# The column of negated maxima turned into a row: float32 transposes in place of float32 products with the identity

## What is computed

```
xn = _layernorm(x, gamma_media, beta_media)          # x: 6404 context rows
ln = _layernorm(latents, gamma_lat, beta_lat)        # 1024 rows
q = ln @ Wq + bq
kv = jnp.concatenate([xn, ln], axis=1) @ Wkv + bkv
...
q = q * DH ** (-0.5)
sim = jnp.einsum('bhid,bhjd->bhij', q, k)
attn = jax.nn.softmax(sim, axis=-1)
out = jnp.einsum('bhij,bhjd->bhid', attn, v)
```

## Time and profile before

| | |
|---|---|
| three runs, us | 1800.03, 1803.17, 1798.9 |
| median of the runs | 1800.03 us |
| profiled execution, first to last instruction | 1800.5 us |
| busy: PE, DVE, ACT, POOL | 96%, 82%, 62%, 15% |
| instructions | 31558, of them PE 9304 matmuls and 9304 weight loads |
| chain that ended last | PE 89%, DVE 5%, ACT 3%, issue 3% |

### The profile page before, as it was taken

One profiled execution on the slowest core, in us unless ns is written; L12 is line 12 of the kernel. 1 busy time (PEld: TensorE's weight loads), 2 busy tenths in 40 slices (PEclk: granted clock), 3 DMA queues, 4 the chain that ended last, 5 costly groups with the idle time before them and its releaser, 6 DMA issues.

```text
span 1800.5 us, 31558 instructions
## 1 busy us (share of the span) xinstructions
PE 1734.3 (96%) x9304; PEld 869.9 (48%) x9304; DVE 1477.0 (82%) x2386; ACT 1109.2 (62%) x1362; POOL 270.0 (15%) x352
## 2 busy tenths in 40 slices
PE   6978999999999999999999999999999999999997
PEld 4854444444444444444444444444444444445764
DVE  7968988888888888887879797978888888876677
ACT  4555666666666666666666666666666666676554
POOL 4746992000000000000000000000000000001444
PEclk8989999999999999999999999999999999999999
DMA  5001210000000000000000000000000000001000
GB/s 167 2 1 36 71 40 1 0 0 0 0 0 0 0 0 0 0 0 0 0 0 0 0 0 0 0 0 0 0 0 0 0 0 1 0 1 35 2 2 13
DMA packets 17753, 16.68 MB, mean 9 GB/s; under 512 B 6047, under 2 KB 15907, under 8 KB 17318
## 3 DMA queue, kind: packets, MB, share of 16 engines
q1 hardware_dynamic: 17446, 15.48, 2.8%
q0 software_dynamic: 256, 0.53, 0.1%
HBM read 13.95 MB, written 2.06 MB: 9 GB/s over the span
## 4 chain that ended last, share of the span: by engine, by line
PE 89%; DVE 5%; ACT 3%; issue 3%; POOL 0%; DMA 0%; SPq 0%; DVEq 0%; POOLq 0%; ACTq 0%
PE PS L1782 89%; ACT p_arena L963 1%; DVE mxs L1363 1%; DVE mxs L1636 1%; ACT p_arena L956 0%; DVE z_arena L1677 0%; DVE w_arena L1144 0%; DVE w_arena L1318 0%; DVE acc L1682 0%; ACT z_arena L799 0%; POOL w_arena L605 0%; PE PS L1791 0%; DMA vecs<-in_L_attn_b_conv_w 0%; POOL z_arena L737 0%; SPq L416 0%
## 5 line engine op out<-in xcount | busy, mean ns | idle before, releaser
L953 ACT ACTIVATE p_arena<-PS 128x1024 f16<-128x1024 f32 (+1 forms) x480 | 484.8, 1010 | 523.1 <-PE PS L1782 522.8
L1782 PE MATMUL PS<-p_arena,z_arena 128*128 128x512 f16 (+1 forms) x2896 | 748.3, 374 | 1.4 <-ACT p_arena L963 0.3
L1782 PE MATMUL PS<-a_arena,z_arena 128*128 (+1 forms) x2832 | 746.4, 380 | 1.5 <-DVE a_arena L1651 1.4
L1395 DVE TENSOR_TENSOR p_arena<-p_arena 128x1024 f16<-128x1024 f32 (+1 forms) x480 | 574.5, 1197 | 99.9 <-ACT p_arena L956 89.2
L1363 DVE TENSOR_REDUCE mxs<-PS 128x512 f32 (+1 forms) x900 | 582.0, 667 | 86.5 <-PE PS L1782 83.1
L956 ACT ACTIVATE p_arena<-PS 128x1024 f32<-128x1024 f32 (+1 forms) x480 | 481.6, 1003 | 0.0
L1782 PEld LDWEIGHTS PS<-a_arena,z_arena 128*128 (+1 forms) x2832 | 274.9, 98 | 328.9 <-issue 2.0
L1782 PEld LDWEIGHTS PS<-p_arena,z_arena 128*128 (+1 forms) x2896 | 275.8, 98 | 313.2 <-ACT p_arena L963 8.8
L1782 PE MATMUL PS<-z_arena,a_arena 128*128 (+3 forms) x1024 | 353.4, 360 | 10.4 <-DVE mxs L1363 8.1
L717 POOL IOTA a_arena<- 128x512 f16 x1 | 0.6, 558 | 1289.7 <-DVE acc L1406 1289.7
L1782 PEld LDWEIGHTS PS<-z_arena,a_arena 128*128 (+1 forms) x1024 | 97.8, 98 | 143.7 <-DVE mxs L1363 26.2
(11 more groups left out here) (337 smaller groups left out, 1006.7 us busy)
## 6 DMA issues: line engine op xcount, KB each, us to landing
w_arena<-in_L_ffn_gate_up_w SPq DMA_DIRECT2D x8, 512.0 KB, 3.6
p_arena<-in_ctx SPq DMA_DIRECT2D x2, 1600.0 KB, 9.1
w_arena<-in_L_ffn_down_w SPq DMA_DIRECT2D x8, 256.0 KB, 3.9
a_arena<-in_L_xattn_Wkv SPq DMA_DIRECT2D x1, 1024.0 KB, 6.0
xg_dram<-VO SPq DMA_DIRECT2D x1, 975.0 KB, 8.2
w_arena<-in_x SPq DMA_DIRECT2D x1, 512.0 KB, 4.2
a_arena<-in_L_xattn_Wo SPq DMA_DIRECT2D x1, 512.0 KB, 6.8
w_arena<-in_L_xattn_Wq SPq DMA_DIRECT2D x1, 512.0 KB
```

The lines of the kernel that those rows point to most:

```text
L953: s.activation(Phi[:, r % 3, 0:w], ps, ACT.Exp, scale=1 / SSC).then_inc(hi_ready, 1)
L1395: v.tensor_tensor(Plo[:, r % 3, at:w], P32[:, r % 2, at:w], Phi[:, r % 3, at:w], ALU.subtract).then_inc(lo_ready, 1)
L1782: return t.matmul(o, l, r, start=start, stop=stop)
```

## The change

The four products in `max_to_row` become four transposes, with the same operands and the same place in the stream. Semaphores, banks and every other instruction stay as they are.

```
--- before.py
+++ after.py
@@ -2106,7 +2106,7 @@
             def max_to_row(b):
                 pe.wait_ge(m_neg, b + 1)
                 for i in range(4):
-                    last = mm(PS[0:1, row_bank(b), i * P:(i + 1) * P], mcol[:, 1, i:i + 1], I32[:])
+                    last = t.transpose(PS[0:1, row_bank(b), i * P:(i + 1) * P], mcol[:, 1, i:i + 1], I32[:])
                 last.then_inc(m_row, 1)
 
             def project(b, k):
```

## The result

The changed kernel takes 1788.84 us (median of six runs, 1786.69 to 1790.51) against 1799.96: a ratio of 0.9936, 95% interval 0.9925 to 0.9946, or 11.1 us less. The forecast was 1793.6 with a range of 1790.0 to 1797.5. The sign was right, the gain was 1.7 times what was forecast, and the time lies outside the range.

What follows compares the result with a forecast made beforehand. PE was taken to bound the kernel; 15 groups of four calls, each falling from 0.215 to 0.108 us, gave -6.4 us with the edges left unchanged, so 1793.6 us from the 1800.03 median, range 1790.0 to 1797.5.

Steps and rivals of the forecast that it cites:

- What bounds the kernel, and that the gain would stay: In the 13-block stretch PE is busy 1211.66 of 1219.00 us; its 0.43 us gain per block should stay.
- Removed and added: In the 15 groups, 120 matmul records become 60; each call falls from 0.215 to 0.107 us, -6.4 us in all.
- The edges "I leave as they are": Around each group, about 0.2 us beyond streaming should stay; at most they go, adding 3.0 us to the gain.
- narrow transposes are slow: Rival: one-column transposes may not load ahead, 0.356 us a call, +8.3 us, 1808.3 us; chance 0.06.
- One pass: Rival: each transpose call costs 0.054 us, -9.7 us, 1790.4 us; chance 0.07, shared with edges gone.
- The mode does nothing: Rival: PE runs the transpose as the float32 product, two halves, 0.215 us a call, 1800.0 us; chance 0.07.
- The 4x of the Trainium skill: Transpose mode 4x faster for float32: a call from 0.215 to 0.054 us, -9.7 instead of -6.4 us; not adopted.
- DVE's row addition: Line 1376, waiting 0.39 us for the group, can start 0.38 us earlier; its idle time should stay 0.3 to 0.4 us.

Runs made afterwards that it cites:

- e8: Changed kernel with each of the four transposes made twice, eight per group: 1797.05 us, ratio 0.9980 to the kernel before.
- e2: Kernel before, float32 products kept, the column repeated 128 times as stationary operand: 1796.24 us, ratio 0.9978 to before.
- e4: Kernel before, four float32 products replaced by eight one-column float16 products on a high and low part: 1793.54 us, ratio 0.9956 to before.
- e9: Kernel before, float32 products kept, the column repeated 64 times as stationary operand: 1801.43 us, ratio 0.9999 to before.
- e3: Changed kernel, transposes with the column repeated 128 times as stationary operand: 1790.39 us, ratio 0.9940 to the kernel before.
- e5: Changed kernel with the first of the four calls a float32 product again: 1795.08 us, ratio 0.9970 to the kernel before.
- e6: Changed kernel with the last of the four calls a float32 product again: 1795.28 us, ratio 0.9969 to the kernel before.
- e11: The kernel before, repeated unchanged for a second profile of its head and tail: 1800.23 us, ratio 1.0000.

## Why the prediction was wrong

- *What bounds the kernel, and that the gain would stay:* right. PE's own waits stayed at 5.7 us, and doubling the group (e8) costs 0.1095 us for each transpose, all of it in the end.
- *Removed and added:* right. 120 records became 60, pitch 0.108 as before, call 0.215 to 0.107; streaming fell by 0.43 us a group as summed.
- ***The edges "I leave as they are":* this is the step that failed.** I read them correctly, 0.2 us a group, put them down to the one-column operand, and concluded that they stay because the operand keeps its one column. The condition was incomplete. They belong to *products* with a narrow stationary operand (e2, e4, e9) and not to float32 transposes with the same operand (the changed kernel, e3, e8; e5 and e6 have both kinds in one group). The term was set to 0 and measured 15 x 0.205 = 3.1 us; I had written 3.0 as its upper end, gave that case a share of 0.07, and so put it beyond the centre where it should have been the sum: 1800.03 - 9.5 = 1790.5. The transposes of line 2131 have no gap behind them, but with their 128 columns either reading foretells that. The trace had a better row, which I had before me only as a duration: the transpose of line 1793, with 64 columns, starts one pitch after those with 128, its load 0.21 us ahead.
- *The range:* it ended at 1790.0. Even with the edges the median is 1.7 us below, within the scatter of an execution, 1786.7 to 1792.4 for this kernel, of which my 1.0 us took too little account.
- *The rival "narrow transposes are slow"* is out: their loads run 0.22 us ahead. *"One pass"*, at 0.054 us a call: out, by e3 and e8. *"The mode does nothing"*: out, by 60 records in place of 120. The Trainium skill's incompatibility of column tiling and float32 transposes (TensorEngine Tiling, Gotcha 2) does not cost anything here, and another rule of that page fits the edges better: changing the tiling mode drains the engine (Key Properties). That a product with 1 or 64 columns is such a change of mode, from and back to the full array, is my reading; the page doesn't say it of a product for which no tile was asked. Taken together with Gotcha 2, a float32 transpose with few columns would then stay in the full array, and one with few rows would not. The runs and the rows of lines 1793 and 1794 agree with this, 0.1 us or a little more for each change, but no trace names a mode, and another cause with the same borders is not excluded.
- *The 4x of the Trainium skill* (TensorE: Matmul & The Clock Gate, Terms): measured 2x in streaming. The total, with the edges, is 1.07 to 0.45 us, 2.4x.
- *DVE's row addition:* I forecast 0.38 us of advance and then asked for an idle time of 0.3 to 0.4 us to remain, which contradicts it. The check was wrong, and the advance, 0.46 us from the scores' start (344.10 - 341.54 before, 339.70 - 337.60 after), is set by DVE as I had it: line 1376 no longer waits for PE at all; it starts when line 1395 is through (338.56 + 1.22 = 339.78, with starts overlapping by 0.08). Its margin has moved to the reciprocal, whose wait for PE fell from 0.3 to 0.16 us a block. By these waits, an estimate: PE time taken from that stretch beyond another 0.16 us would run into DVE.

## What to carry to other kernels

Read the time of a small group of instructions from the end of its neighbour before to the start of its neighbour behind, not from its own pitch: here a fifth of the group lay in the two gaps. Where a weight load starts with its matmul and not 0.2 us ahead, PE lost about 0.1 us at each such border here; ask what changes there, and treat "it stays" as a guess that needs a price in the range. For turning a few columns into a row, `transpose` with float32 was the best of the forms tried, ahead of a float16 pair that streams as long.

## What the runs showed of the hardware that was not expected

- A product with 1 or 64 stationary columns between products with 128 costs about 0.1 us of PE at each border (gap 0.10 to 0.11 ahead, 0.09 to 0.1 behind), in float32 and with one column in float16, once for a run of them. With 128 columns it costs none. Products with 128 columns and one row show the same gap ahead, 0.09 us. A float32 transpose with one column costs none beside 128-column products, and the border between it and a narrow product does (0.095 us); one with two rows, seen twice, costs 0.13 us ahead.
- Padding the stationary operand of such products to 128 columns by a broadcast operand saved 0.18 us a group, although each load went from 84 to 190 ns.
- After an idle time of PE of 2.35 us, the same program kept granted clock 1.00 in one execution (e11) and fell to about 0.5 for some 3 us in another, after which its tail was 1.6 us longer.
